# Scratch rows for queries and keys: each part stored as often as it is used, and one load for 48 rows in place of three

## The reference

```
Q, K, V = (proj(Wq), proj(Wk), proj(Wv))
Q1, Q2 = jnp.split(Q, 2, axis=-1)
K1, K2 = jnp.split(K, 2, axis=-1)
A1 = jnp.where(causal, jnp.einsum('bhnd,bhmd->bhnm', Q1, K1) * scaling, -jnp.inf)
A2 = jnp.where(causal, jnp.einsum('bhnd,bhmd->bhnm', Q2, K2) * scaling, -jnp.inf)
attn = jax.nn.softmax(A1, axis=-1) - lam * jax.nn.softmax(A2, axis=-1)
O = jnp.einsum('bhnm,bhmd->bhnd', attn, V)
```

## Time and profile before

| | us |
|---|---|
| median of three timed runs | 497.31 |
| lowest, highest | 493.74, 498.1 |
| span of the profiled execution, first to last instruction | 495.9 |
| mean granted TensorE clock | 0.990 |

### The profile page before, as it was taken

How to read it: one execution, slowest core, us unless ns; L and a number is a source line. 1 busy time by engine, 2 the same in 40 slices (tenths; PEclk the granted TensorE clock), 3 DMA queues, 4 the chain that set the end, 5 groups by cost and what they waited for, 6 DMA issues and landing times.

```text
span 495.9 us, 8638 instructions
## 1 busy us (share of the span) xinstructions
PE 456.9 (92%) x3072; PEld 220.1 (44%) x3072; DVE 398.5 (80%) x812; ACT 281.5 (57%) x456; POOL 269.4 (54%) x237
## 2 busy tenths in 40 slices
PE   2999988869999999999999999999889998989995
PEld 2855446434444435453454444444434444423332
DVE  1634457987988988899999996978999899986785
ACT  2264663445766834638885545556685446567640
POOL 6322350224555773746674449636575864546982
PEclk9999997998999999999999999999999999999999
DMA  7900037683563630152337573023462462304201
GB/s 272 338 15 0 22 105 145 115 155 111 124 109 92 115 56 5 34 122 64 111 86 155 113 101 89 1 63 89 127 146 71 101 118 63 71 3 110 62 2 42
DMA packets 49891, 46.16 MB, mean 93 GB/s; under 512 B 6360, under 2 KB 39480, under 8 KB 49208
## 3 DMA queue, kind: packets, MB, share of 16 engines
q1 hardware_dynamic: 49848, 45.61, 38.9%
HBM read 37.47 MB, written 7.60 MB: 91 GB/s over the span
## 4 chain that ended last, share of the span: by engine, by line
PE 72%; DVE 18%; ACT 3%; DMA 2%; issue 2%; POOLq 1%; POOL 1%; SPq 0%; DVEq 0%; ACTq 0%
PE bank L782 10%; PE bank L773 9%; PE bank L794 7%; PE scores L813 7%; PE bank L868 5%; DVE nmax L1332 3%; PE scores L708 3%; PE scores L699 3%; PE scores L723 3%; PE scores L702 3%; PE scores L807 3%; DVE h L1308 3%; PE scores L747 3%; PE bank L873 2%; DVE h L1315 2%
## 5 line engine op out<-in xcount | busy, mean ns | idle before, releaser
L1133 POOL TENSOR_TENSOR gb<-gb,wb 128x512 f32<-128x512 f32 x64 | 84.3, 1319 | 97.5 <-ACT gb L1021 83.9
L1036 ACT ACTIVATE pk<-scores 128x1024 f32<-128x1024 f32 x96 | 95.3, 1023 | 41.3 <-PE scores L813 41.0
L1126 POOL TENSOR_SCALAR_AFFINE_SELECT pk<-pk 128x512 f32<-128x512 f32 (+1 forms) x96 | 81.8, 860 | 40.7 <-ACT pk L1036 40.2
L1332 DVE TENSOR_REDUCE nmax<-scores 128x8 f32<-128x1024 f32 x64 | 76.5, 1217 | 9.5 <-PE scores L813 8.9
L1018 ACT ACTIVATE gt<-bank,bgh 128x512 f32<-128x512 f32 (+1 forms) x68 | 46.7, 687 | 63.8 <-PE bank L773 52.0
L782 PE MATMUL bank<-xnt,wu 128*128 128x512 f32 x128 | 68.4, 616 | 2.3 <-DVE h L1315 2.2
L773 PE MATMUL bank<-xnt,wg 128*128 128x512 f32 x128 | 70.3, 632 | 0.0
L794 PE MATMUL bank<-h,wd 128*128 128x512 f32 x128 | 66.5, 617 | 0.0
L1308 DVE SCALAR_TENSOR_TENSOR h<-gt,gb 128x512 f32<-128x512 f32 x64 | 58.4, 913 | 4.3 <-PE bank L794 3.1
L1315 DVE SCALAR_TENSOR_TENSOR h<-bank,bu,h 128x512 f32<-128x512 f32 x64 | 48.1, 751 | 11.2 <-PE bank L782 9.2
L1137 POOL TENSOR_TENSOR orms<-oms,minus_half 128x32 f32<-128x32 f32 x8 | 44.7, 5584 | 10.3 <-DVE oms L1362 10.3
(11 more groups left out here) (262 smaller groups left out, 708.9 us busy)
## 6 DMA issues: line engine op xcount, KB each, us to landing
wb<-wt_scratch SPq DMA_DIRECT2D x64, 256.0 KB, 4.2
parts_scratch<-parts SPq DMA_DIRECT2D x48, 128.0 KB, 2.3
qa<-parts_scratch SPq DMA_DIRECT2D x32, 96.0 KB
ka<-parts_scratch SPq DMA_DIRECT2D x32, 96.0 KB
qa<-parts_scratch SPq DMA_DIRECT2D x32, 64.0 KB
ka<-parts_scratch SPq DMA_DIRECT2D x32, 64.0 KB
ha<-in_wkq SPq DMA_DIRECT2D x1, 1024.0 KB, 5.0
wb<-in_wvo SPq DMA_DIRECT2D x1, 1024.0 KB, 8.5
```

Source lines behind the costliest of these rows:

```text
L1036: A(dst.rearrange("p (h m) q -> p m h q", m=2), pairs[pair_of(step)][:, :, :].rearrange("p m (h q) -> p m h q", q=cols), ACT.Exp, scale=SC ...
L1126: pool.affine_select(out=dst, in_=dst, compare_op=ALU.is_ge, fill=0.0, base=0, pattern=[[0, heads], [1, P]], channel_multiplier=-1).then_i ...
L1133: pw(gb[:, c % 2, :], gb[:, c % 2, :], wb[:, k % 2, j % 2, :], ALU.mult).then_inc(s_ga_done, 1)
L1332: V.tensor_reduce(dst, src, AX, ALU.max, negate=True).then_inc(s_nmax_done, 1)
```

## The change

The scratch tensor has all six rows of terms for each of the 8 elements of a component, in the last but one place: `(CHUNKS, 2, HEADS, 2, DH, 6, CHUNK)`. A store writes its part to every row that uses it, three, two or one, by repeating the source. A fetch loads the 48 rows of one component for a half of the heads in one DMA. The rows' order within the 48 changes from part by part to element by element, for queries and keys alike.

```diff
+TERMS_OF = ((slice(2, 5), slice(0, 6, 5), slice(1, 2)), (slice(0, 3), slice(3, 6, 2), slice(4, 5)))
...
-QK_IN = 16 * 2 * 6
+QK_IN = 16 * 2 * 2
...
                                 done, name = ((s_part1, "part1"), (s_part2, "part2"), (s_part3, "part3"))[a]
+                                terms = TERMS_OF[n][a]
                                 for f in range(2):
-                                    r = a if n == 0 else 2 - a
                                     sp.wait_ge(done, at(c, name, 2 * n + f + 1))
-                                    dst = t["parts_dram"][c, n, f * 2 * GH:(f + 1) * 2 * GH, :, r * DH:(r + 1) * DH, :]
-                                    sp.dma_start(dst, parts[:, a, 2 * n + f, :]).then_inc(s_parts_stored[f], 16)
+                                    dst = t["parts_dram"][c, n, f * 2 * GH:(f + 1) * 2 * GH].rearrange("h m d w t -> (h m d) w t")
+                                    src = parts[:, a, 2 * n + f, :].unsqueeze(1)
+                                    sp.dma_start(dst[:, terms, :], src.to_broadcast([P, len(range(TERM_PAIRS)[terms]), CHUNK])).then_inc(
+                                        s_parts_stored[f], 16)
...
                                 for m in range(2):
-                                    row = m * HALF
-                                    for width in (3, 2, 1):
-                                        first = 0 if n == 0 else 3 - width
-                                        src = t["parts_dram"][c, n, heads, m, first * DH:(first + width) * DH, b * SEQ:(b + 1) * SEQ]
-                                        sp.dma_start(dst[row:row + width * DH, b, heads, :],
-                                                     src.rearrange("h r t -> r h t")).then_inc(s_qk_in[b][f], 16)
-                                        row += width * DH
+                                    src = t["parts_dram"][c, n, heads, m].rearrange("h d w t -> (d w) h t")
+                                    sp.dma_start(dst[m * HALF:m * HALF + TERMS, b, heads, :],
+                                                 src[:, :, b * SEQ:(b + 1) * SEQ]).then_inc(s_qk_in[b][f], 16)
...
-    t["parts_dram"] = nc.dram_tensor("parts_scratch", (CHUNKS, 2, HEADS, 2, 3 * DH, CHUNK), BF16, kind="Internal").ap()
+    t["parts_dram"] = nc.dram_tensor("parts_scratch", (CHUNKS, 2, HEADS, 2, DH, TERM_PAIRS, CHUNK), BF16, kind="Internal").ap()
```

More of the change, by code:

```diff
@@ L38 @@
 SCALE1 = 1.0 / float(np.sqrt(DH))
-TERMS = 6 * DH
+TERM_PAIRS = 6
+TERMS = TERM_PAIRS * DH
+TERMS_OF = ((slice(2, 5), slice(0, 6, 5), slice(1, 2)), (slice(0, 3), slice(3, 6, 2), slice(4, 5)))
 MROWS = TERMS + 2
```

## The result

The changed kernel takes 493.05 us in the median of 13 runs (491.07 to 494.64), the kernel before 497.31 us (493.74 to 500.58); the ratio is 0.9927, with a 95% interval of 0.9901 to 0.9953. In a later set of 11 runs it was 0.9921 (0.9888 to 0.9954). By the ratio the gain is 0.7%, 3.6 us: small but sure. The profiled span went from 495.9 to 491.9 us.

The account below looks back on a forecast made before the run. TensorE, busy 92% of the 495.9 us span, was taken to bound the kernel. Loads -1.2 us and stores +0.8 us gave -0.4 us: 496.9 us against a 497.31 us median, own range 495 to 498.5, eight in ten 492.5 to 502.5.

Parts of the forecast that it names:

- What the loads give back: Chunk 0's first minus step: the DMA queue empties sooner, so TensorE waits less for the minus rows, -1.2 us.
- the half-busy tail: End of the fetch ahead of the minus rows: 2.4 us with half the engines done, 1.2 us if spread over 16.
- the bound of 3.0: Largest gain at the minus step: the whole 2.00 us wait plus 1.0 us from the VectorE instruction at 111.54.
- Why the loads are quicker: Fetches: 48 rows lie evenly on 16 engines, three each; loads of 24, 16 or 8 cannot.
- The stores: Chunk 0: doubled bytes at 273 GB/s start the first fetch 3.5 us later; TensorE's first masks wait 0.8 us.
- Rival 1: Doubled stores at 197 GB/s hold back chunk 0's first fetch: slower, 503 us, chance 0.17.
- rival 4: Repeated source doubles a store's issue time, so chunk 0's first fetch starts near 84: 501.7 us, chance 0.05.
- The issue: SP's issue of a fetch: 24 loads take about 10 us, 8 take 3.0 us; given no price.
- Half a fetch: Loads for one half of the heads, 0.79 MB, land 6.6 us after their first issue.
- Rival 3: Rows per engine never mattered, each packet takes 50 ns: +2.9 us in chunk 0, 500.2 us, chance 0.12.
- Rival 2: Evenly spread 512-byte rows speed up to 27 ns; no chunk 0 stall, full 3.0 us at minus step: 494.3 us, chance 0.20.

Follow-up runs that it names:

- e7: The changed kernel with 2.5 MB of useless HBM to HBM copies behind the second wb broadcast of chunk 0: 501.19 us, 1.0092 of before.
- e3: The kernel before with twelve useless matmuls put ahead of TensorE's wait for the minus rows of chunk 0: 496.85 us, 1.0019 of before.
- e2: The changed kernel with each 48-row load cut into three even loads of 16 rows: 497.39 us, 1.0031 of before.
- e1: The changed kernel with each 48-row load cut again into loads of 24, 16 and 8 rows: 496.61 us, 1.0018 of before.
- e6: The changed kernel with the minus rows of component 0 issued by ScalarE, those of component 1 by SP: 491.91 us, 0.9911 of before.
- e4: The changed kernel with 1.5 MB of useless HBM to HBM copies behind the second wb broadcast of chunk 0: 494.60 us, 0.9965 of before.
- e10: The same kernel as e6, timed beside the changed kernel: 491.73 us, 0.9899 of before.
- e9: The kernel before run again, unchanged: 497.74 us in its one run.
- e5: The kernel before with four part rows in the scratch, three loads of 16 rows and 16 stores a chunk instead of 12: 498.46 us, 1.0030 of before.

## Why the prediction was right, and where it was not

The forecast was a gain of 0.4 us; measured were 3.6 us of the timed time and 4.0 us of the span. The way was right, "within 1%" holds, and 493.05 lies in the range of eight in ten, 0.55 us above its lower end; the forecast's own range, 495 to 498.5, was missed. The picture holds that in chunk 0 transfers count at the first fetch and at the minus step, and that the loads of the later chunks stay hidden. The size is off by a factor of nine, and that the wide range still holds is in part luck: one term was too small, one was missing, one cost did not come, and the reason given for the gain is not what the runs show.

*What the loads give back (-1.2 us).* The place was right. But I priced only the half-busy tail, as the queue being empty 1.2 us sooner; GpSimd's wait for the `wb` pair behind the fetch ends 3.7 us sooner. So the whole wait of 2.00 us went, and the VectorE instruction took 1.07 us for 1.67: 1.8 us in the table, between the 1.2 and the bound of 3.0 (whose 1.0 us for that instruction is 0.76 by its own rows). What takes the gain past the bound is a term that the sum did not have, the half clock behind the idle time, 1.84 us in these two traces. The row for it could have been had from the trace of before; I read that stretch for waits only. That the idle time is its cause rests on three traces with and nine without, and on e7; that the changed kernel runs less at half clock stands in its timed runs too, but e3's show no gain from filling the wait.

*Why the loads are quicker.* The prediction said: because 48 rows lie evenly on 16 engines. (That 16 rows do so too it overlooked; e2 is built on it.) Even loads of 16 rows took 8.5 us for half a fetch and uneven ones 8.4 us, one load for each component 6.4 to 6.7, so at the first fetch it is fewer loads that help. Behind the second fetch e1 and e2 again agree (16.3 and 16.5 us), and both lie between before (18.4) and the changed kernel (15.0). No run shows a share of evenness, and a small one could hide behind e2's slower issue; what the first 2 us there are due to is open.

*The stores (+3.5 us at the fetch, +0.8 us for TensorE).* The rate was outside my bounds: 340 GB/s, not 197 to 273. I had scaled 197 GB/s by the share of 0.72; after the change the same window has 340 at a share of 1.03, so more bytes were moved for the same busy time as well. The fetch starts 1.0 us later and half of it takes 1.4 to 1.8 us less, so it does not land later: the first masks of the max step stand at 84.93 against 84.98 before. The wait of +0.8 us is not there in the traces of the two kernels, but its place is real: TensorE waits 1.1, 1.7 and 1.3 us there in e6, e4 and e10, which are the changed kernel up to that point, and 0.2 us in e9. In e1 and e2, where the loads are three again, the later start is not paid back, and the wait is 3.1 and 1.6 us. So the doubled stores are free only together with the single load. The later chunks, for which 2.2 us later were forecast, show nothing: the fetches of chunks 1 and 2 start at 129.04 and 254.22 where they started at 132.90 and 257.99, 3.8 us sooner, which is the kernel's lead. Rival 1 is out for this kernel, and rival 4 with it: twelve stores take SP 8.84 us instead of 8.13.

*The issue (no price).* This step failed in its reasoning, not in the sum's sign. "Nothing hangs on the difference" between 3 and 10 us is wrong, as the `wb` pair in SP's queue behind the fetch shows. At n = 27 the kernel before loses 0.16 us on the changed one in its first trace and 0.61 us in e9; with a slower issue, in e2, it is 1.25 us.

*Half a fetch.* 6.6 us were forecast, and this was right: where TensorE waits for it, the wait ends 6.4, 6.6 and 6.7 us after the first issue (e6, e10, e4); before, 8.2 us (e9). Rival 3 (50 ns for each packet whatever the shape) is out in its result, since the minus wait did go and the half fetch is not 8.7 us long. Rival 2 came nearest in time (494.3 us), by another way than it said: 193 GB/s at a share of 1.21 is no faster for one packet (51 ns by the same sum, 1.21 x 16 x 512 / 193) than the 50 ns of before. There are only more of them under way. The rule of the Trainium skill ("DMA: Bandwidth & Descriptors", section "Specifications") that pieces from 512 bytes up move at an engine's full rate, about 27 GiB/s, is not borne out by either kernel: 161 and 193 GB/s over 16 engines are 10 and 12 GB/s for each, with rows of 512 bytes.

## What to carry to other kernels

Price a wait of TensorE by what stands behind it too: look at the granted clock of the next 4 us before you write down that 2 us of idle time cost 2 us. Count a queue twice, once as bytes on the DMA engines and once as issue time on SP, and for each ask which small transfer stands behind it; three even loads were as slow as three uneven ones here. And in a kernel with a written-out order, look up the same instruction in both traces: the steps in its distance tell within 0.1 us where time was made. Count both from the span's start, read the list of waits from the span's start too and not from a late window, and take more than one trace of each kernel: a wait that one execution hides behind a slow front stands open in the next.

## What the runs showed of the hardware

- An idle time of TensorE of 2.0 and 2.5 us amid dense work was followed, 1.5 and 1.1 us after its end, by half clock (0.56 and 0.60 in windows of 3.9 and 3.6 us) though TensorE was busy all through; in an idle time of 6.1 us the clock fell before its end. With the idle time filled, 0.3 us long or absent, the clock stayed whole there (nine traces). At chunk 0's first fetch waits of 1.3, 1.7, 3.1 and 3.6 us were followed by half clock, waits of 1.1 and 1.6 us were not.
- Half a fetch, 0.79 MB in rows of 512 bytes, took 6.4 to 6.7 us in four loads of 48 rows and 8.4 to 8.5 us in twelve, whether these had 16 rows each or 24, 16 and 8 (7.8 us in e5).
- The busy share of the DMA engines goes over 1.00 (1.21 in the fetch): packets overlap on an engine, so a share near 1 is no proof that it cannot take more.
- Stores of rows of 1 KB from 128 partitions reached 340 GB/s, loads of rows of 512 bytes onto 48 partitions 193 GB/s.
- SP's time for one issue depends on its shape and not simply on its size: about 0.37 us in the mix of 24, 16 and 8 rows, 0.46 us for 16 rows, 0.4 to 0.5 us for 48 rows, 0.8 us for the 3 minus rows.
